# A new job order for the four engines in the preparation stage of a fused attention and expert kernel

## What is computed

```python
q = x @ Wqa @ Wqb                     # Wqa 256x64, Wqb 64x(16*192)
ckv = x @ Wkva                        # 64 latent channels and 64 rotary ones
compressed, k_pe = (ckv[..., :KV_RANK], ckv[..., KV_RANK:])
kv = compressed @ Wkvb                # keys and values of 16 heads from 64 channels
q_pe = _rope(q_pe)
k_pe = _rope(k_pe)
...
out = jnp.einsum('bhnm,bhmd->bhnd', attn, v)
return out @ Wout
```

## Time and profile before

| what | value |
|---|---|
| median of 3 runs | 1632.64 us (1631.37 to 1638.89) |
| the profiled execution, its own time | 1635.59 us |
| its span, first to last instruction | 1633.5 us |
| granted TensorE clock, mean | 0.988 |
| busy: PE, DVE, POOL, ACT | 94%, 71%, 57%, 49% |
| first instruction of the attention stage on PE | 71.47 us |

### The profile page before, as it was taken

The page is one execution under the profiler, slowest core; times in us unless marked ns, Lnnn a source line. Parts: engine busy times, 40 slices in busy tenths (PEclk is TensorE's granted clock), DMA queues, the critical chain, the costliest instruction groups (busy, mean ns, idle before and its releaser), DMA issues. The chain is left out here.

```text
span 1633.5 us, 68004 instructions
## 1 busy us (share of the span) xinstructions
PE 1533.4 (94%) x29424; PEld 1279.1 (78%) x29424; DVE 1160.9 (71%) x2609; ACT 801.9 (49%) x1725; POOL 928.2 (57%) x783
## 2 busy tenths in 40 slices
PE   5679999999999999999999899997899999999998
PEld 4568777877777878777887778886688888888887
DVE  6768887888778888887888778888554455445442
ACT  6645555555555555555555455554343333333332
POOL 4366676767676766676767676765343442342322
PEclk9889999999999999999999999999799999999999
DMA  8422211122222112322122212112521222122020
GB/s 302 129 76 65 71 48 43 46 58 61 75 69 75 42 49 62 88 55 68 53 59 63 68 55 56 36 36 87 147 65 44 87 72 78 46 71 87 25 84 13
DMA packets 98936, 114.98 MB, mean 70 GB/s; under 512 B 37520, under 2 KB 61840, under 8 KB 98640
## 3 DMA queue, kind: packets, MB, share of 16 engines
q1 hardware_dynamic: 98640, 110.65, 23.5%
HBM read 78.74 MB, written 15.07 MB: 57 GB/s over the span
## 5 line engine op out<-in xcount | busy, mean ns | idle before, releaser
L1468 ACT ACTIVATE probs<-aps,nmax 128x896 f32<-128x896 f32 (+7 forms) x512 | 378.1, 740 | 411.9 <-DVE nmax L1516 400.1
L1516 DVE CUSTOM_DVE_ANT_0 aps<-aps,mask_row 128x896 f32<-128x896 f32 (+7 forms) x512 | 380.8, 759 | 123.2 <-PE aps L47 119.5
L1194 POOL TENSOR_TENSOR rot<-rot,sinT 64x512 f32<-64x512 f32 x126 | 160.4, 1273 | 294.2 <-DMA rot<-rot 294.2
L47 PE MATMUL aps<-kTh,qh 128*128 128x512 f32 (+3 forms) x768 | 290.4, 378 | 16.1 <-DVE ql L1203 7.2
L47 PE MATMUL aps<-pT_second,vrep 32*64 32x128 f32 (+1 forms) x15616 | 265.2, 261 | 24.8 <-issue 21.6
L1939 POOL TENSOR_TENSOR sg<-sg,mass_b 128x512 f32<-128x512 f32 x88 | 114.8, 1304 | 291.1 <-ACT sg L1837 290.8
L47 PEld LDWEIGHTS aps<-pT_second,vrep 32*64 32x64 f32 x15616 | 225.7, 131 | 65.1 <-issue 52.4
L1526 DVE STREAM_TRANSPOSE pT_second<-probs 128x896 f32<-128x896 f32 (+3 forms) x256 | 264.0, 1032 | 5.5 <-ACT probs L1468 5.3
L47 PE MATMUL aps<-kTl,qh 128*128 128x512 f32 (+3 forms) x768 | 259.2, 345 | 0.5 <-issue 0.3
L1885 DVE TENSOR_TENSOR act_sb<-fps,sg 128x512 f32<-128x512 f32 x88 | 60.6, 689 | 230.3 <-PE fps L47 179.6
L47 PE MATMUL aps<-kTh,ql 128*128 128x512 f32 (+3 forms) x768 | 222.6, 344 | 0.0
(11 more groups left out here) (198 smaller groups left out, 2903.8 us busy)
## 6 DMA issues: line engine op xcount, KB each, us to landing
rot<-rot SPq DMA_DIRECT2D x256, 64.0 KB
linv_b<-inverses_scratch SPq DMA_DIRECT2D x128, 128.0 KB, 3.0
mass_b<-mass_scratch SPq DMA_DIRECT2D x64, 256.0 KB, 3.9
wqs<-wq_scratch SPq DMA_DIRECT2D x30, 256.0 KB, 3.5
mass_b<-mass_scratch SPq DMA_DIRECT2D x48, 96.0 KB, 4.0
raw_numbers<-in_x SPq DMA_DIRECT2D x8, 512.0 KB, 6.6
vrep<-values_scratch SPq DMA_DIRECT2D x16, 256.0 KB, 4.4
inverses_scratch<-linv_t SPq DMA_DIRECT2D x256, 1.0 KB
```

Source lines behind the costliest of these rows:

```text
L47: return nc.tensor.matmul(out, lhsT, rhs, start=start, stop=stop, skip_group_check=True)
L1194: eng.tensor_tensor(rot2[:, k, :], rot2[:, k, :], t.sinT[:, cols], ALU.mult).then_inc(q_turned, 1)
L1468: nc.scalar.activation(probs[:, SLOT[x, r], 0:w], sps[:, at:at + w], ACT.Exp, bias=nmax[:, c, a, j:j + 1], scale=-1.0, accum_out=lsum[:, c ...
L1516: nc.vector.tensor_tensor_reduce(out=s, in0=s, in1=mask[:, N - PW[c][j]:N], scale=-1.0, scalar=3.0e38, op0=ALU.add, op1=ALU.min, accum_out ...
```

## The change

The same 52 jobs of PE, 66 of DVE, 62 of ACT and 24 of POOL stand in another order on each engine; no job is added, removed or changed, and the SP queue's list is untouched. Two lines of the lists as a sample, the last of `VECTOR`:

```diff
-                  PL(11), QL(0, 1), PL(12), R1(1, 0), PL(10), XL(1, 1, 1), R2(1, 0), QL(1, 0), PL(13),
-                  R2(1, 1), R1(1, 1), QL(1, 1), PL(14), PL(15)]
+                  R2(0, 1), R1(0, 1), RL(), XL(1, 0, 1), QL(0, 1), XL(1, 1, 1), R2(1, 0), R1(1, 0), PL(12), PL(13),
+                  R1(1, 1), R2(1, 1), PL(9), QL(1, 0), PL(14), PL(11), QL(1, 1), PL(10)]
```

More of the change, by code:

```diff
@@ L194, in attention_prepare @@
[L194 to L200, removed]
@@ L201, in attention_prepare @@
-        POOL = [RS(2, 0), RS(2, 1), RS(3, 0), RS(3, 1), KA(2, 0), KL(2, 0), KA(2, 1), KL(2, 1), RS(0, 1),
-                RS(0, 0), KA(3, 0), KA(3, 1), KL(3, 0), KL(3, 1), RS(1, 1), RS(1, 0), KA(0, 0), KL(0, 0),
-                KA(0, 1), KL(0, 1), KA(1, 0), KL(1, 0), KA(1, 1), KL(1, 1)]
+        TENSOR = [TX(2, 1, 0), TX(2, 0, 0), TX(2, 1, 1), TX(3, 1, 0), PJ(2, 0, "q"), TX(2, 0, 1), TX(3, 0, 0), PJ(2,
+                  0, "k"), PJ(2, 1, "q"), PJ(2, 1, "k"), PJ(3, 0, "q"), TX(3, 1, 1), PJ(3, 0, "k"), TX(3, 0, 1), PJ(3,
+                  1, "q"), TV(2), TX(0, 1, 1), PJ(3, 1, "k"), PR(1), PR(3), TX(0, 0, 0), PR(4), PR(5), TX(0, 1, 0),
+                  PR(6), PR(2), TV(3), PR(15), PR(0), PJ(0, 0, "k"), TX(0, 0, 1), PR(8), PJ(0, 0, "q"), PR(7), PJ(0,
+                  1, "k"), TX(1, 1, 0), TX(1, 0, 0), PR(12), PJ(0, 1, "q"), PR(13), PR(9), TX(1, 0, 1), TX(1, 1, 1),
+                  PJ(1, 0, "k"), PJ(1, 0, "q"), TV(0), PJ(1, 1, "k"), PJ(1, 1, "q"), PR(14), PR(11), TV(1), PR(10)]
@@ new lines, in attention_prepare @@
+        VECTOR = [ST(2, 0), INL(), ST(2, 1), ST(3, 0), ST(3, 1), XL(2, 0, 0), XL(2, 1, 0), XL(2, 1, 1), XL(3, 1, 0),
+                  QL(2, 0), XL(2, 0, 1), R2(2, 0), R1(2, 0), XL(3, 0, 0), R2(2, 1), R1(2, 1), QL(2, 1), ST(0, 1),
+                  XL(3, 1, 1), XL(3, 0, 1), ST(0, 0), QL(3, 0), R2(3, 0), XL(0, 1, 1), R2(3, 1), R1(3, 1), R1(3, 0),
+                  PL(1), PL(3), XL(0, 0, 0), PL(4), PL(5), XL(0, 1, 0), PL(6), PL(2), ST(1, 0), QL(3, 1), PL(15),
+                  XL(0, 0, 1), ST(1, 1), R1(0, 0), PL(0), QL(0, 0), PL(8), XL(1, 1, 0), PL(7), XL(1, 0, 0), R2(0, 0),
+                  R2(0, 1), R1(0, 1), RL(), XL(1, 0, 1), QL(0, 1), XL(1, 1, 1), R2(1, 0), R1(1, 0), PL(12), PL(13),
+                  R1(1, 1), R2(1, 1), PL(9), QL(1, 0), PL(14), PL(11), QL(1, 1), PL(10)]
@@ new lines, in attention_prepare @@
+        SCALAR = [INH(), NM(2, 0), XH(2, 1, 0), XH(2, 0, 0), NM(2, 1), NM(3, 0), XH(2, 1, 1), XH(3, 1, 0), XH(2, 0,
+                  1), QH_(2, 0), XH(3, 0, 0), NM(3, 1), KH(2, 0), QH_(2, 1), QH_(3, 0), XH(3, 1, 1), KH(2, 1), XH(3,
+                  0, 1), NM(0, 1), VO(2), XH(0, 1, 1), NM(0, 0), PH(1), PH(3), XH(0, 0, 0), PH(4), PH(5), XH(0, 1, 0),
+                  PH(6), PH(2), KH(3, 1), KH(3, 0), VO(3), QH_(3, 1), PH(15), XH(0, 0, 1), PH(0), PH(8), NM(1, 0),
+                  QH_(0, 0), PH(7), XH(1, 1, 0), XH(1, 0, 0), NM(1, 1), RH(), XH(1, 0, 1), KH(0, 0), QH_(0, 1), XH(1,
+                  1, 1), PH(12), KH(0, 1), QH_(1, 0), PH(13), PH(9), VO(0), KH(1, 0), QH_(1, 1), PH(14), PH(11), KH(1,
+                  1), PH(10), VO(1)]
@@ L204, in attention_prepare @@
+        POOL = [RS(2, 0), RS(2, 1), RS(3, 0), RS(3, 1), KA(2, 0), KL(2, 0), KA(2, 1), RS(0, 1), KL(2, 1), RS(0, 0),
+                KA(3, 0), KA(3, 1), KL(3, 0), RS(1, 0), RS(1, 1), KL(3, 1), KA(0, 0), KA(0, 1), KL(0, 0), KL(0, 1),
+                KA(1, 0), KA(1, 1), KL(1, 0), KL(1, 1)]
         COUNT = {}
```

## The result

The changed kernel takes 1640.96 us (median of 22 runs, 1636.17 to 1647.12); the kernel before, beside it, 1634.24 us (22 runs). The ratio is 1.0035, with a 95% interval of 1.0022 to 1.0047: **5.7 us slower** (3.6 to 7.7), less than the 0.5% I had called the bound of what can be told, but outside the range of 1628 to 1639 and on the other side from any gain.

A forecast was written before the change was run, and what follows sets the result against it. POOL's key chain was taken to bound the preparation's end, with SP 0.25 us ahead. Block end -0.35 plus attention start +0.4 summed to 0 against the profiled 1635.6 us; the median was put at 1633.0, range 1628 to 1639.

The forecast's parts named there:

- the bound of what can be told: Whole kernel: a measurement can tell about 0.5% (8.2 us) from no change; chance of no change 0.93.
- `RL` (1.4): DVE, preparation: `RL`'s term in the 30.2 us of jobs left from `R2(3,1)` at 37.4.
- The walk: Preparation: new job lists carried forward job by job with durations read from the old trace; error taken as 0.5 us.
- the walk breaks on DVE: Rival, preparation: ACT's wait for key stores, PE at half clock or late `XH` delays DVE; +1 to +3, chance 0.2.
- over 1 us of waits after 38: DVE, preparation: sign that the forecast's mechanism is wrong; the walk found no wait over 0.1 us there.
- The tail of the SP queue: Preparation's end: pair 7's store waits for `PL(10)`, lands 2.0 us later, then two value stores; Block ends 0.3 to 0.4 earlier.
- the threshold I had given (2.35): SP queue: pair 7's landing time in us above which the slow-store rival decides against the forecast; that rival's chance 0.13.
- The gain of 3.2 us: Computing engines, preparation's end: 1.7 from DVE's waits, 1.5 from the key chain; rival that it arrives, chance 0.12.
- the 67.6: DVE, preparation: forecast end in us of its last job, 37.4 + 30.2, against 69.3 before.
- The start of attention: First scores on PE: idle 5.7 us instead of 2.9, so query products run at half clock; +0.4 us.
- The bound of 0.9: Start of attention: upper bound in us on the half-clock cost, four times 0.21; lower bound 0.
- The keys' stores: ACT, preparation: `QH_(1,0)` needs batch 3's keys landed near 59.5; wait of some 0.4 us, hidden by 0.8 us at `PL(13)`.

The follow-up runs named there:

- e4: Changed kernel with `RL` three jobs earlier on DVE, ahead of POOL's jobs, and `RH` one job earlier on ACT: 1633.56 us, ratio 1.0005 to the kernel before.
- e7: Kernel before with two more GpSimd tensor_tensor jobs, reading SBUF, put beside `RL`, which stays in place: 1635.35 us, a single run.
- e1: Changed kernel with `RL` back right ahead of `R2(3,1)` on DVE and `RH` behind `VO(2)` on ACT: 1639.24 us, ratio 1.0026 to the kernel before.
- e6: Kernel before with heads 10 and 15, and 11 and 14, exchanged so `PL(10)` is DVE's last job: 1637.72 us, ratio 1.0017 to the kernel before.
- e5: Changed kernel with `RL` ahead of POOL's jobs and the stored heads early: 1632.41 us, ratio 0.9984 to the kernel before.
- e2: Changed kernel with heads 12 and 13 exchanged for 9, 10 and 11, so stored heads come early: 1636.65 us, ratio 1.0014 to the kernel before.
- e3: Changed kernel with `RL` back right ahead of `R2(3,1)` and the stored heads early: 1633.62 us, ratio 1.0002 to the kernel before.
- e8: Kernel before with three GpSimd memsets, writing SBUF without reading it, put beside `RL`, which stays in place: 1630.54 us, a single run.

## Why the prediction was right and wrong

**The step that failed** is the term "`RL` (1.4)" in the sum of DVE's jobs, "`RL` 37.60 - 36.24 = 1.36". The duration was read correctly, from a place where POOL had only just finished a `KA` and then had nothing to do. The new place has POOL's longest unbroken stretch beside it, and there `RL` takes 4.9 us (e4 and e7 show both directions). The walk held each job's duration as a property of the job; for this one it is a property of its neighbour on another engine. Nothing else on DVE in this stage was hit so: nearly all its other jobs have at most one input in SBUF, and they took the same time in both kernels (each `XL` 657 to 692 ns). Only `INL` has two as well, and it runs at the start, ahead of POOL's first rotation.

**What followed from it** was named as a rival, "the walk breaks on DVE", with 0.2 and +1 to +3. Of the 5.1 us by which DVE ended later than forecast, `RL` is 3.5, and the waits of 0.66 and 1.10 us for PE's results at half clock are 1.8; the two make up all of it, and 0.2 us more. With `RL` out of POOL's way both are gone (e4), so the second is a consequence of the first: PE sat idle while `RL` blocked the `XL` that its next jobs need. The rival was right in kind, too small in size, and its causes were the wrong ones. The prediction's own sign against itself, over 1 us of waits after 38, is there with 2.0 us, but the larger loss is in none of these waits: the blocked instructions stand in the profile as busy time.

**The tail of the SP queue** was right: pair 7 waits for DVE's last job, and landing plus two issues stand behind it. Its landing was seen after 2.34 us against the 2.0 I took (2.3 in e1 and e4 too, but 2.0 in e6; why was not settled). That is the threshold I had given (2.35) at which SP would no longer be ahead of what POOL had set before, and e4's 71.40 is indeed level with the 71.47 of the earlier trace rows.

**The gain of 3.2 us** on the computing engines was there to be had: in e4 DVE ends at 67.63 and POOL at 67.62. That DVE's end fits the 67.6 to the hundredth is luck: e4's trace had `R2(3,1)` start at 36.95 and not at 37.4, and DVE then waited 0.68 us for ACT and 0.17 more, which the walk had not; in e5 the same stretch, as long, ends at 68.26. That the tail eats it is shown from both sides, by e2 and e5 (taking it away gives 3.5 and 2.4 us at the first scores, 3.1 in both at the start of attention as seen from DVE's end) and by e6 (adding it costs 2.0).

**The start of attention**: +0.4 forecast, 0.5 measured. The size was right; the reason I gave, the longer idle time, is not the whole one, since e3, e5 and e7 pay the same without it. (The bound of 0.9 in the prediction, four times 0.21, should have been 0.84.)

**The keys' stores**: I expected a wait of 0.4 us on ACT, and found 2.46; 1.4 of it is that they landed 6.3 us after issue and not 4.9. In the changed kernel `RL` hid it; in e1 it came to the surface. Why the same stores take 4.9, 5.3 or 6.4 us from kernel to kernel was not settled. The stores issued right behind them do not explain it: e4 and e5 have these and land after 5.2 to 5.3, the changed kernel has none until 61.20 and takes 6.3.

**The sum over all**: at the first scores the changed kernel is 5.5 us behind that before, and the measured 5.7 us (3.6 to 7.7) is that. The stages behind it took no part that the runs can show: the two traced executions differ by 8.1 us in span, 1641.6 against 1633.5, but from one execution to the next those stages vary by as much as the rest (e1, with first scores at 84.40, has a span of 1632.6). The range was too narrow on the slow side because all its cases were built from the same walk: they had no case in which an instruction itself gets longer.

## What to carry to other kernels

When an order of work is changed, check each moved instruction against its new neighbours on the other engines, not only its dependencies: on VectorE, look for instructions with two inputs in SBUF, and see what GpSimd does at the new time. Where one instance has its normal duration and its twin a several times longer one, suspect blocking, and see whose instruction ended just ahead of the long one's end. And look at what the DMA queue still has to wait for behind the last job of a stage: exchanging which heads came last left DVE's time as it was (30.7 and 30.6 us from `R2(3,1)` to its end in e4 and e5), and took 2.4 to 3.5 us off the first scores (e4 to e5, changed to e2).

## What the runs showed of the hardware that I had not expected

- A VectorE `scalar_tensor_tensor` with both inputs in SBUF was kept waiting for whole GpSimd `tensor_tensor` instructions: 2632 ns for one that takes 288, 1627 for one that takes 546. It did not get in at the seam between GpSimd's second and third job at 57.7, though it had been waiting since 56.5.
- The blocked ones ended at a fixed distance behind the end of a GpSimd instruction: 0.15 us for 128x128 (59.16 behind 59.01 in the changed kernel, 58.42 behind 58.27 in e2, 37.66 behind 37.51 in e7), and 0.42 us for 128x384 (60.71 behind 60.29, 60.43 behind 60.01, 39.21 behind 38.79).
- GpSimd memsets of the same total length (2.40 us for three) did not slow it at all: 1.43 us.
- With 2.3 to 2.9 us of idle time on TensorE ahead of the attention stage, the six query products ran at full clock in one kernel (e2, 1.63 us), partly at full and partly at half in two (before, 2.16; e8, 2.71), and at half in three (e3, e5, e7, 2.90). What decides it was not settled.
- The same four DMA stores, with 512, 512, 512 and 256 KB in the same order, had their last landing 4.9 to 6.4 us after issue, depending on the kernel. The store of pair 7, with no other in flight, landed after 2.0 us in the kernel before and e6, and after 2.3 in the changed kernel, e1 and e4.
